# Attention on one Trainium2 core: projection units on other steps of a batch, and the normed input and its low parts on other engines

## The reference

```python
h   = group_norm(x, 32 groups) * gn_w + gn_b             # (8, 512, 1024)
qkv = einsum('oc,bcn->bon', qkv_w, h) + qkv_b            # 1536 output channels
att = softmax(q^T k / 8)                                 # per batch and head, 1024 x 1024
out = einsum(att, v);  out = proj_w @ out + proj_b
x   = x + out
# layer 1: q, k, v of the 256 top positions, LayerNorm, softmax, their v replaced, projection, x + out
```

## Time and profile before

| | before |
|---|---|
| median of 3 runs | 3378.47 us (3378.28 to 3380.99) |
| the profiled execution | 3384.99 us, of which 3383.0 us are the profile's span |
| TensorE (PE) busy | 2937.5 us, 87% |
| VectorE (DVE) busy | 2124.9 us, 63% |
| ScalarE (ACT) busy | 1588.4 us, 47% |
| GpSimd (POOL) busy | 443.2 us, 13% |
| mean granted clock of TensorE | 0.934 of full speed |

### The profile page before, as it was taken

How to read it: one execution, slowest core, us unless ns; L and a number is a source line. 1 busy time by engine, 2 the same in 40 slices (tenths; PEclk the granted TensorE clock), 3 DMA queues, 4 the chain that set the end, 5 groups by cost and what they waited for, 6 DMA issues and landing times. The chain is left out here.

```text
span 3383.0 us, 34913 instructions
## 1 busy us (share of the span) xinstructions
PE 2937.5 (87%) x12368; PEld 2375.9 (70%) x12368; DVE 2124.9 (63%) x3224; ACT 1588.4 (47%) x1935; POOL 443.2 (13%) x193
## 2 busy tenths in 40 slices
PE   4998998999899999989998998999755877777877
PEld 2776886788688778868876786888544666656656
DVE  5686767768776776777677677757624435435443
ACT  2565656556564555656456555646521222212221
POOL 1012111100210120021012002011101100111000
PEclk8999999999899999989999999999977988888888
DMA  6222131222123122212312131232030100111100
GB/s 217 60 57 63 54 110 44 63 88 76 57 59 113 48 63 71 84 37 79 113 47 70 53 100 38 82 102 58 19 121 25 50 37 37 37 37 50 43 31 25
DMA packets 131084, 221.52 MB, mean 65 GB/s; under 512 B 50048, under 2 KB 50304, under 8 KB 130432
## 3 DMA queue, kind: packets, MB, share of 16 engines
q1 hardware_dynamic: 130944, 219.69, 21.1%
HBM read 143.34 MB, written 42.21 MB: 55 GB/s over the span
## 5 line engine op out<-in xcount | busy, mean ns | idle before, releaser
L590 DVE TENSOR_REDUCE row_max<-pmax 128x1 f32<-128x512 f32 x1024 | 703.2, 687 | 602.5 <-PE pmax L389 599.0
L484 ACT ACTIVATE p_high<-ring 128x1024 fp32r<-128x1024 f32 x512 | 525.1, 1026 | 730.6 <-PE ring L410 730.4
L606 DVE TENSOR_TENSOR p_low<-p_full,p_high 128x1024 fp32r<-128x1024 f32 x512 | 665.1, 1299 | 6.3 <-ACT p_full L487 6.3
L389 PE MATMUL pmax<-k_high_low,q_high_high 128*128 128x512 f32 x1024 | 459.5, 449 | 98.9 <-DVE row_max L590 96.1
L487 ACT ACTIVATE p_full<-ring 128x1024 f32<-128x1024 f32 x512 | 520.9, 1017 | 0.0
L389 PEld LDWEIGHTS pmax<-k_high_low,q_high_high 128*128 128x128 f32 x1024 | 316.5, 309 | 221.0 <-DVE row_max L590 135.5
L767 POOL TENSOR_TENSOR o_normed<-num_den,o_normed 64x1024 f32<-64x1024 f32 x64 | 173.1, 2705 | 1961.4 <-DMA o_normed<-rec_rows 1943.6
L426 PE MATMUL pv<-p_high,v_high 128*128 128x512 f32 x1024 | 411.9, 402 | 0.0
L427 PE MATMUL pv<-p_high,v_low 128*128 128x512 f32 x1024 | 406.9, 397 | 0.0
L344 PE MATMUL fill<-h_high,w_high 128*128 128x512 f32 x768 | 309.2, 403 | 39.4 <-DVE q_low_max L619 17.1
L410 PE MATMUL ring<-q_low_max,k_high_one 65*128 65x512 f32 x1024 | 330.9, 405 | 1.9 <-DMA q_low_max<-row_max_top 1.9
(11 more groups left out here) (161 smaller groups left out, 3748.6 us busy)
## 6 DMA issues: line engine op xcount, KB each, us to landing
x_tiles<-in_x SPq DMA_DIRECT2D x64, 512.0 KB, 5.4
w_high<-w_split SPq DMA_DIRECT2D x128, 256.0 KB, 2.9
w_low<-w_split SPq DMA_DIRECT2D x128, 256.0 KB, 2.9
k_high_one<-k_high_low SPq DMA_DIRECT2D x128, 128.0 KB, 2.3
q_high_high<-q_high_high SPq DMA_DIRECT2D x128, 128.0 KB, 2.3
o_normed<-rec_rows SPq DMA_DIRECT2D x64, 256.0 KB, 3.5
x<-x_tiles SPq DMA_DIRECT2D x32, 512.0 KB, 3.5
x_full<-x SPq DMA_DIRECT2D x32, 512.0 KB, 3.3
```

The lines of the kernel that those rows point to most:

```text
L389: mm(pmax[:, :], q1[:, q_slot(h), first:first + HALF - 3:4], k1[:, k_slot(h), n * HALF:(n + 1) * HALF], start=True, stop=True).then_inc(s_ ...
L484: nc.scalar.activation(ph[:, r, :], ring[:, r, :], ACT.Exp, scale=ATT_SCALE).then_inc(s_ph, 1)
L590: nc.vector.reduce_max(mcol[:, h % 2, n, i:i + 1], pmax[:, :], AX_X).then_inc(s_mx, 1)
L606: tt(pl[:, r, :], p32[:, r, :], ph[:, r, :].bitcast(F32), ALU.subtract).then_inc(s_pl, 1)
```

## The change

- **Other steps for the units.** A table gives each unit its step. In heads 0 and 1 of a batch, k, the first half of v and the second half of q are whole units, so that step 0 to 2 of head 0 carry a whole unit each, q is in its steps 6 and 7, and the seven steps from (1, 1) are all "o" units; the eighth is at (2, 0). In the other pairs every q, k and v unit is spread. The group sums g have the steps (4, 2) and (4, 5) to themselves, no "vt" shares a step with the end of another unit, and heads 4 and 5 have no whole unit.
- **The normed input.** ScalarE norms x in place in (5, 1) to (5, 4) and copies it to `h_high` in (5, 5) to (6, 0); VectorE subtracts for `h_low` in (5, 6) to (6, 1). VectorE's norming and GpSimd's subtraction are gone. In the preamble the same for batch 0.
- **The output.** `o_low` is subtracted by VectorE in step 0 of the odd heads. GpSimd keeps `normalise` and `rstd`.
- **Statistics** go from (4, 1) to (4, 4) to (3, 1) and (3, 3) to (3, 5), `group_scale` from (5, 2) to (5, 0). The last store of a batch, and the loads for the residual, are issued one step earlier.

```diff
+PAIR_STEPS = (begins(0, 1, 6, 8, 2, 3, 3, 5, whole=(("k", 0), ("k", 1), ("v", 0), ("q", 1))),
+              begins(1, 3, 5, 8, 10, 12, 12, 14),
+              begins(0, 3, 6, 8, 10, 12, 12, 14),
+              begins(2, 4, 6, 8, 10, 12, 12, 14))
...
         if kind == 0 and g > 0:
-            for s in range(5):
-                put(b, 3 + s, o[s])
-            for s in range(3):
-                put(a + 2, s, o[5 + s])
+            for s in range(7):
+                put(b, 1 + s, o[s])
+            put(a + 2, 0, o[7])
...
         if kind == 2 and b0 + 1 < BATCH:
-            put(a, 6, ("g", b0 + 1, 0))
-            put(b, 0, ("g", b0 + 1, 1))
+            put(a, 2, ("g", b0 + 1, 0))
+            put(a, 5, ("g", b0 + 1, 1))
...
-            def normed(b, t):
+            def normed_full(b, t):
+                act.wait_ge(s_gab, b + 1)
                 a, c = gs[:, 6, t:t + 1], gs[:, 7, t:t + 1]
-                nc.scalar.activation(hh[:, t, :], xs[:, t, :], ACT.Identity, bias=c, scale=a).then_inc(s_hh, 1)
+                nc.scalar.activation(xs[:, t, :], xs[:, t, :], ACT.Identity, bias=c, scale=a).then_inc(s_h32, 1)
+
+            def normed_high(b, t):
+                if b > 0 and t >= 1:
+                    act.wait_ge(s_unit, unit(("v", PAIRS * b - 1, 1)))
+                act.wait_ge(s_h32, bt((b, t)))
+                nc.scalar.activation(hh[:, t, :], xs[:, t, :], ACT.Copy).then_inc(s_hh, 1)
...
-            def normed_full(b, t):
+            def normed_low(b, t):
                 dve.wait_ge(s_hh, bt((b, t)))
-                dve.wait_ge(s_gab, b + 1)
-                nc.vector.tensor_scalar(xs[:, t, :], xs[:, t, :], gs[:, 6, t:t + 1], gs[:, 7, t:t + 1],
-                                        ALU.mult, ALU.add).then_inc(s_h32, 1)
+                tt(hl[:, t, :], xs[:, t, :], hh[:, t, :].bitcast(F32), ALU.subtract).then_inc(s_hl, 1)
+
+            def o_low(g):
+                dve.wait_ge(s_on, 2 * g + 2)
+                dve.wait_ge(s_oh, g + 1)
+                tt(ol[:, g % PAIRS, :], on[:, :], oh[:, g % PAIRS, :].bitcast(F32), ALU.subtract).then_inc(s_ol, 1)
...
+                if h % 2 == 1 and h > 1 and s == 0:
+                    o_low(h // 2 - 1)
```

More of the change, by code:

```diff
@@ L106, with begins @@
 HALF_UNITS = (0, 1)
+def begins(k0, k1, q0, q1, v0, v1, vt0, vt1, whole=()):
+    begin = {("k", 0): k0, ("k", 1): k1, ("q", 0): q0, ("q", 1): q1, ("v", 0): v0, ("v", 1): v1}
+    return {**{u: (s, u in whole) for u, s in begin.items()}, ("vt", 0): vt0, ("vt", 1): vt1}
+PAIR_STEPS = (begins(0, 1, 6, 8, 2, 3, 3, 5, whole=(("k", 0), ("k", 1), ("v", 0), ("q", 1))),
+              begins(1, 3, 5, 8, 10, 12, 12, 14),
+              begins(0, 3, 6, 8, 10, 12, 12, 14),
+              begins(2, 4, 6, 8, 10, 12, 12, 14))
 def parts_by_step():
@@ L125, in parts_by_step @@
             o = [("o", b0 - 1, t, i) for t in range(CT) for i in range(2)]
-            for s in range(5):
-                put(b, 3 + s, o[s])
-            for s in range(3):
-                put(a + 2, s, o[5 + s])
+            for s in range(7):
+                put(b, 1 + s, o[s])
+            put(a + 2, 0, o[7])
         if n == ALL_PAIRS:
             continue
[L132 to L152, removed]
+        begin = PAIR_STEPS[kind]
+        for name, i in (("k", 0), ("k", 1), ("q", 0), ("q", 1), ("v", 0), ("v", 1)):
+            at_step, whole = begin[name, i]
+            (put if whole else spread)(a + at_step // STEPS, at_step % STEPS, (name, n, i))
+        for i in range(2):
+            at_step = begin["vt", i]
+            put(a + at_step // STEPS, at_step % STEPS, ("vt", n, i))
         if kind == 2 and b0 + 1 < BATCH:
-            put(a, 6, ("g", b0 + 1, 0))
-            put(b, 0, ("g", b0 + 1, 1))
+            put(a, 2, ("g", b0 + 1, 0))
+            put(a, 5, ("g", b0 + 1, 1))
     return at
@@ L553, in step @@
                 b = h // HEADS + 1
-                if h % HEADS == 5 and b < BATCH and 3 <= s <= 6:
-                    normed(b, s - 3)
+                if h % HEADS == 5 and b < BATCH and 1 <= s <= 4:
+                    normed_full(b, s - 1)
+                if h % HEADS == 5 and b < BATCH and s >= 5:
+                    normed_high(b, s - 5)
+                if h % HEADS == 6 and b < BATCH and s == 0:
+                    normed_high(b, CT - 1)
                 if h % 2 == 0 and h > 0 and s == 7:
@@ L751, in _ @@
             reciprocal(ALL_HEADS - 1)
+            o_low(ALL_PAIRS - 1)
             for u in EPILOGUE:
@@ L763, in normalise @@
                 if a == 1:
-                    if h > 1:
-                        pool.wait_ge(s_ol, h // 2)
-                    pool.wait_ge(s_hl, bt((min((h + 3) // HEADS, BATCH - 1), CT - 1)))
+                    pool.wait_ge(s_rstd, min((h + 3) // HEADS + 1, BATCH))
                 nc.gpsimd.tensor_tensor(on[rows, :], nd[rows, a, :], on[rows, :], ALU.mult).then_inc(s_on, 1)
[L769 to L772, removed]
-                                        ALU.subtract).then_inc(s_ol, 1)
             def rstd(b):
                 pool.wait_ge(s_gst, gst((b, "var")))
+                if b > 0:
+                    pool.wait_ge(s_on, HEADS * (b - 1) + 4)
                 nc.gpsimd.tensor_tensor(gs[:, 5, :], gs[:, 4, :], gs[:, 0, :], ALU.pow).then_inc(s_rstd, 1)
-            def h_low(b, t):
-                pool.wait_ge(s_h32, bt((b, t)))
-                nc.gpsimd.tensor_tensor(hl[:, t, :], xs[:, t, :], hh[:, t, :].bitcast(F32),
-                                        ALU.subtract).then_inc(s_hl, 1)
             pool.wait_ge(s_dset, 1)
             rstd(0)
-            for t in range(CT):
-                h_low(0, t)
             for h in range(1, ALL_HEADS):
@@ L792, in _ @@
                 normalise(h - 1)
-                if h % HEADS == 5 and b < BATCH:
-                    for t in range(CT):
-                        h_low(b, t)
-                if h % 2 == 0:
-                    o_low(h // 2 - 1)
             normalise(ALL_HEADS - 1)
-            o_low(ALL_PAIRS - 1)
         @block.sync
```

29 lines of the change are left out of this document (14 added, 15 removed).

## The result

| | before | after |
|---|---|---|
| median | 3378.38 us (3375.32 to 3380.99, 4 runs) | 3266.95 us (3263.96 to 3270.79, 4 runs) |
| ratio, 95% interval | | 0.9671 (0.9654 to 0.9688) |
| profiled execution | 3384.99, span 3383.0 | 3269.11, span 3267.3 |
| mean granted clock | 0.934 | 0.947 |

The kernel became 3.3% faster, 111 us. The forecast was 3237 in a range of 3205 to 3278, so it fell inside the range, but outside the narrower 3220 to 3260 that had the chance of 0.60, and the gain was over-estimated by 30 us in the medians; in the profiled executions 139 us were expected and 115.7 found.

The account below looks back on a forecast made before the run. TensorE was taken as the bound, fed badly at one place in the batch. Gains of 132 us in seven batches, about 4 in the last, 2 in the preamble and 1.4 at the end, total 139, gave 3237, range 3205 to 3278.

Parts of the forecast that it names:

- The prices of the steps: Every head: an empty, half or whole step, by unit work carried, takes 3.13, 4.15 or 5.51 us.
- The extras: VectorE's other work in a step: a half step hides 1.85 us, an empty one about 0.5; the rest costs time.
- The division: `normalise` on GpSimd, once a head, can hold `p_low` about 2.66 us; mostly in slack, so 0.3 added in head 5.
- Head 3: It receives the statistics, 1.6 us of extras in four half steps, all hidden: stays at 32.3 us.
- Seven batches have such a change of batch: 132: Each batch goes from 300.3 to 281.4 us, 18.9 gained, in seven batches.
- The last batch: It has only the gain of heads 0 to 2 and of head 5's whole units, about 4 us.
- The term for `o_low`: On VectorE it costs 1.2 us, against 2.66 on GpSimd: 1.4 gained at the end; priced in odd heads' step 0.
- The preamble: Four `h_low` on GpSimd become ScalarE norming and copying with the subtraction alongside: 1 to 3 us gained, 2 taken.
- the clock falls all the same: From (5, 6) to (6, 1) TensorE still drops to 1.2 GHz: 5 us a batch, 35 in all, 3272; chance 0.13.
- The rule of the Trainium skill: Two-SBUF-input VectorE and SBUF-reading GpSimd instructions exclude each other; `normalise` could cost 10 us a batch, giving 3309.
- The extras are hidden: Half steps make good VectorE's lateness in empty steps: 25 us more gained, 3212, or 3187 if all; chance 0.22.
- The signs: No unit's buffer wait, `p_low` never over 3.5 us, maxima waits some 50; wrong if (4, 2), (5, 7), (6, 0) reach 5.

Follow-up runs that it names:

- e1: The kernel before with the change's step table, statistics and scale steps, but norming, `h_low` and `o_low` on their old engines: 3326.13 us, ratio 0.9823.
- e2: The kernel before with its old step table, but ScalarE norms and copies and VectorE does the `h_low` and `o_low` subtractions: 3328.91 us, ratio 0.9839.
- e9: The kernel before with the second group sum in (5, 0) put ahead of the q unit, not behind it: 3364.18 us, ratio 0.9948.
- e4: The changed kernel with `h_low` alone back on GpSimd: 3290.04 us, ratio 0.9713.
- e7: As e6, with the division of a head's output on VectorE, one or two steps later, and `o_high` and `o_low` moved too: 3234.46 us, ratio 0.9568.
- e6: The changed kernel with the statistics in (2, 2), (2, 4), (3, 1) and (3, 3): 3257.42 us, ratio 0.9631.
- e8: The changed kernel with the units of pair 1, in heads 0 and 1 of batch 0, spread instead of whole: 3263.63 us, ratio 0.9662.
- e5: The changed kernel with `o_low` alone back on GpSimd: 3265.01 us, ratio 0.9656.
- e10: e7 with three divisions a step later, in heads 5, 6 and 7, and `o_high` later in heads 5 and 7: 3212.8 us, ratio 0.9499.
- e3: The kernel before with the second group sum in (4, 7) instead of (5, 0): 3380.4 us, ratio 0.9993.

## Why the prediction was right in kind and too large in size

- **The bound** was read rightly: TensorE, fed badly at the change of batch. The two parts of the change, steps and engines, are each half of the gain (e1, e2). The two causes named at the change of batch are each shown by themselves, and each is smaller than a half: the order of two buffers was worth 19 us in the kernel before (e9), the subtraction on GpSimd 14 to 23 in the changed one (e4).
- **The prices of the steps** held. By head of batch 1, forecast and measured: 37.0 and 36.8; 44.1 and 44.1; 34.5 and 34.9; 32.3 and 34.5; 33.2 and 33.0; 35.0 and 34.1; 32.5 and 32.5; 32.8 and 33.1. Without head 3 the sum is off by 0.6 us in 249. In part this is luck, two errors with opposite signs. The extras cost less than priced: (4, 3) and (4, 6) take 4.8 in the mean, 0.7 each over a half step where 1.0 was priced, and (5, 6) and (5, 7) together 6.9, 0.3 over where 1.6 was priced. The division cost more: (4, 7) takes 4.7 and (5, 5) 4.9, 0.5 and 0.7 over a half step, and both are back at 4.15 in e7, where 0.3 was priced in head 5 and nothing in head 4.
- **Head 3 was mis-sized.** "They are hidden ... 32.3" counted the statistics against the slack of a half step, and the division on GpSimd nowhere in this head. The division lands on (3, 4) and (3, 5), where the slack is then already used. Head 3 took 34.9 in the mean, 2.6 more than forecast, some 15 us in six batches; about 0.5 of the 2.6 is the q low part of (2, 7), which was priced in head 2 and is paid in (3, 0). In the mean e6 gave back 1.5 and e7 another 0.8.
- **The division was the term priced too low:** 0.3 us a batch, "most of that lies in steps with slack". Taking it off GpSimd was worth 23 us in e7, some 3 a batch.
- **"Seven batches have such a change of batch: 132"** failed for batch 0, which gained 11.9 and not 18.9. Heads 0 to 2 got 2 us slower (98.4 to 100.7) where a gain was counted, and head 3 2.8 slower. The seven empty steps that the new table leaves in head 1, which the expectation of e8 blames, are not the reason: heads 0 and 1 together fell from 66.9 to 66.2, and e7 has the same empty steps and takes 97.2 for heads 0 to 2. The loss is in (2, 7), with 6.2 us, where the division met `row_max_top`:

```profile
179.06 2.40 POOL L780 TENSOR_TENSOR o_normed<-num_den,o_normed 64x1024 f32<-64x1024 f32 x1 [34.19 <-DMA o_normed<-rec_rows]
179.67 1.82 DVE L605 TENSOR_TENSOR row_max_top<-row_max 128x4 fp32r<-128x4 f32 x1
...
183.27 0.63 PE L386 MATMUL pmax<-k_high_low,q_high_high 128*128 128x512 f32 x1 [1.82 <-DVE row_max L597]
```

- **The last batch**, "about 4", gained 0.4. Its heads 0 to 2 took 0.3 us more than before and head 3 took 2.2 more (31.9 to 34.1), though it has no statistics. Here too the division is the likely cause: it held a `row_max_top` for 1.87 us at (2, 6) and a `p_low` for 3.29 at (0, 5), and in e7 heads 0 to 2 take 114.9 against 117.9 and head 3 takes 32.5.
- **The term for `o_low`** was nothing inside the batch and 1.4 at the end; e5 bears out the first. At the end what follows the last batch became 1.4 us shorter, but only 1.0 of it is this wait: TensorE waited 13.7 us for the last `o_low` on GpSimd (before, e1, e5) and 12.6 or 12.7 for it on VectorE (e2, e8 and the changed kernel). The preamble gave 2.4 for 2, and single profiles differ by about a microsecond: the new preamble ends at 85.5 to 87.2 us in eight of them (86.3 in the mean), the old one at 87.4 to 88.2 in four (87.9).
- **The rival "the clock falls all the same"** has its time (3272) nearer to the 3267 measured than the forecast, but it is out: the granted clock is 1.00 in heads 5 and 6 of all seven changes of batch. The rule of the Trainium skill that names the exclusion (SBUF — State Buffer, Who interferes with whom) is borne out by e4 and e7. What the prediction drew from it, that `normalise` goes on blocking, was right and was priced at a tenth of what it cost.
- **"The extras are hidden"** came about in part, as above, and the division took back more than that gave.
- **The signs:** no unit waits for a q unit's buffer (0.4 us in the preamble is left), the longest `p_low` is 3.46 us, (4, 2), (5, 7) and (6, 0) take 3.1, 3.6 and 4.0. The waits for the maxima are 61.4 us, not some 50.

## What to carry to other kernels

When two engines exclude each other over SBUF, count each instruction of the slower one as a possible stall of the other's queue, and compare that with the cost of doing the work on the other. In e7 the divisions cost VectorE 77.8 us and gave it 65 back, and the kernel still became 23 us faster: work of its own stands in a step that one can choose (e10 won another 22 us by choosing better), while a stall of up to 2.1 us (e4) falls where a transfer lets the other engine go. Price a queue's extras by step, against the slack of that very step, and add up everything that can land in it, what comes by DMA included. A double buffer taken in turn makes a unit wait for the reading of the unit two before it, so don't let two units end in one step; but see first what the unit you move itself waits for (e3).

## What was not expected of the hardware

An instruction of VectorE on 4 elements a partition took 3.92 us beside GpSimd and 1.52 in e3, where such a one takes 0.16 when nothing is in its way (L647 in e3): its own length doesn't set the wait. The 3.92 are longer than one GpSimd instruction of the chain (2.8 in the mean) and end where the chain ends, at 598.7: here VectorE's waiting instruction didn't get its turn between two of GpSimd. GpSimd's own subtraction took 2.40 in the mean in e4, where each came by itself, and 2.8 before. The four `h_low` in a chain held VectorE more than the same four some 5 us apart: in batch 1 the granted clock of heads 5 and 6 was 0.86 and 0.95 before and 0.99 and 0.96 in e4. Part of the 0.86 belongs to (5, 1) with its buffer wait, where the clock is 0.83 (559.5 to 569.3 us) and which e4 doesn't have.
